# Cross-attention K and V as split float32r products, a ctx tile read twice through one buffer, and a new order of work on all five queues

## The reference, cut to what matters

```
# layer 0: attention of x over ctx (16 heads of 16), relu projections, row mask, layernorm
q, k, v = relu(x@Wq+bq), relu(ctx@Wk+bk), relu(ctx@Wv+bv)
x  = layernorm(softmax(mask(q k^T / 4)) v + x) * gamma + beta
# layer 1: a Mamba2 block, then cross-attention over the same ctx (8 heads of 32)
zxbcdt = rms(x) @ in_proj                  # 256 -> 1288
xBC = silu(conv4(xBC));  y = scan over t of h = h*decay + u*B, y = h.C
h  = x + rms(y * silu(z)) @ out_proj
q1 = layernorm(h) @ Wq1;  k1 = ctx @ Wk1;  v1 = ctx @ Wv1
out = h + (softmax(q1 k1^T / sqrt(32)) v1) @ Wo
```

## Time and profile before

| | us |
|---|---|
| median of three runs | 1428.14 |
| profiled execution, time | 1427.8 |
| profiled execution, span | 1426.0 |
| TensorE busy | 1329.9 (93%) |
| VectorE busy | 1267.2 (89%) |
| ScalarE busy | 1089.3 (76%) |
| GpSimd busy | 891.7 (63%) |

### The profile page before, as it was taken

One profiled execution on the slowest core, in us unless ns is written; L12 is line 12 of the kernel. 1 busy time (PEld: TensorE's weight loads), 2 busy tenths in 40 slices (PEclk: granted clock), 3 DMA queues, 4 the chain that ended last, 5 costly groups with the idle time before them and its releaser, 6 DMA issues.

```text
span 1426.0 us, 42008 instructions
## 1 busy us (share of the span) xinstructions
PE 1329.9 (93%) x15112; PEld 1160.4 (81%) x15112; DVE 1267.2 (89%) x3050; ACT 1089.3 (76%) x3300; POOL 891.7 (63%) x1125
## 2 busy tenths in 40 slices
PE   4799999999999999999999999999999999999875
PEld 3688888888888888888888888888888888888764
DVE  5799999999999999998899999998989999999872
ACT  3667787887778788778778778877877878877653
POOL 6366666567666666665656766666666665676642
PEclk9999999999999999999999999999999999999997
DMA  5021121211222111122221122211122211201110
GB/s 190 25 66 63 64 72 58 72 51 39 72 72 72 58 50 54 57 72 72 57 71 52 39 72 72 72 57 50 47 63 72 72 58 60 60 26 54 46 46 15
DMA packets 41132, 86.91 MB, mean 61 GB/s; under 512 B 5728, under 2 KB 10976, under 8 KB 40928
## 3 DMA queue, kind: packets, MB, share of 16 engines
q1 hardware_dynamic: 39632, 81.96, 17.9%
q10 hardware_dynamic: 1296, 2.27, 0.5%
HBM read 75.53 MB, written 8.68 MB: 59 GB/s over the span
## 4 chain that ended last, share of the span: by engine, by line
PE 72%; DVE 11%; POOL 8%; issue 4%; DMA 3%; ACT 1%; SPq 1%; POOLq 0%; DVEq 0%; ACTq 0%
PE bank L294 19%; PE bank L397 9%; PE bank L522 8%; POOL PC L1548 6%; PE bank L535 5%; PE bank L354 5%; PE bank L508 4%; PE bank L387 4%; PE bank L573 4%; PE bank L411 4%; DVE stc L957 3%; DMA cU<-in_cT 3%; PE bank L593 2%; PE bank L622 2%; PE bank L445 2%
## 5 line engine op out<-in xcount | busy, mean ns | idle before, releaser
L848 DVE SCALAR_TENSOR_TENSOR ACC<-bank,cw,ACC 128x250 f32<-128x250 f32 (+2 forms) x576 | 270.3, 473 | 10.4
L1548 POOL TENSOR_TENSOR PC<-PC,stc 128x512 f32<-128x512 f32 x128 | 191.1, 1494 | 78.0 <-DVE stc L964 78.0
L1351 ACT ACTIVATE PC<-bank,stc 128x128 f32<-128x128 f32 x512 | 180.9, 380 | 66.8 <-DVE stc L957 66.8
L1188 ACT ACTIVATE PTA<-bank 128x512 f32<-128x512 f32 x256 | 142.2, 599 | 82.3 <-PE bank L391 80.1
L294 PE MATMUL bank<-xnT,wnl 128*128 128x256 f32 x640 | 199.2, 311 | 0.3 <-DVE xnL L783 0.3
L294 PE MATMUL bank<-xnL,wnh 128*128 128x256 f32 x640 | 179.4, 280 | 0.0
L294 PE MATMUL bank<-xnT,wnh 128*128 128x256 f32 x640 | 179.1, 280 | 0.0
L707 DVE TENSOR_REDUCE sta<-bank 128x4 f32<-128x512 f32 x256 | 160.8, 681 | 8.1 <-PE bank L354 5.6
L872 DVE TENSOR_TENSOR_SCAN L<-DB,id 128x1024 f32<-128x1024 f32 x64 | 146.1, 2282 | 0.0
L522 PE MATMUL bank<-wout,Y 128*128 128x256 f32 x512 | 123.9, 386 | 6.4 <-POOL SQ L1526 6.4
L1489 POOL TENSOR_SCALAR stn<-stn 128x1 f32<-128x1 f32 x64 | 15.2, 238 | 173.2 <-ACT junk L1207 173.2
(11 more groups left out here) (182 smaller groups left out, 4247.7 us busy)
## 6 DMA issues: line engine op xcount, KB each, us to landing
DB<-dec_scratch SPq DMA_DIRECT2D x64, 512.0 KB, 4.5
xT<-in_xT SPq DMA_DIRECT2D x32, 256.0 KB, 2.7
cT<-in_cT SPq DMA_DIRECT2D x32, 256.0 KB, 2.9
xt<-in_xt SPq DMA_DIRECT2D x32, 256.0 KB, 2.7
cU<-in_cT SPq DMA_DIRECT2D x32, 256.0 KB, 4.3
...
```

The lines of the kernel that those rows point to most:

```text
L848: e.scalar_tensor_tensor(out=w, in0=t[:, 0:T].rearrange("p (b t) -> p b t", b=NB)[:, :, 0:125 + k], scalar=cw[:, c, k:k + 1], in1=w, op0=A ...
L1188: e.activation(PTA[n % 4][:, :, :], t[:, :].rearrange("p (i k) -> p i k", i=4), ACT.Exp).then_inc(s_eA, 1)
L1351: op = e.activation(PC[n % 5][:, p, :], t[:, p * 128:(p + 1) * 128], ACT.Exp, bias=stc[g % 4][:, 4 * i + p:4 * i + p + 1], accum_out=stc[g ...
L1548: e.tensor_tensor(PC[n % 5][:, :, :], PC[n % 5][:, :, :], stc[g % 4][:, 16 + 4 * i:20 + 4 * i].unsqueeze(2).to_broadcast([128, 4, 128]), A ...
```

## The change

1. `k1` and `v1` become split products of three: weights `wk1h`/`wk1l`, `wv1h`/`wv1l`, data `cUh`/`cUl`. `k1` calls `proj3`; `v1` issues twelve float32r matmuls instead of four float32 ones.
2. `cU` is gone. ctx is still loaded twice per group, both times into the one buffer `cT`: `load_c(g)` for layer 0, and `load_u(g)` three groups behind it (`AHEAD`). ScalarE gets `split_u`, GpSimd `lo_u`.
3. The two weights are split once: ScalarE at its step 2, GpSimd at its step 17. They are staged in `HT`, and `wq1u` in `OT`; three buffers go, and the ring `PC` has four instead of five.
4. `nm` keeps its first instruction; the second is `nw`, which can stand later in the list.
5. `USES` and all five lists are replaced. In the lists of ScalarE, GpSimd and SyncE some offsets are larger by a constant; only the order within a queue counts. `later` on GpSimd now stands before the first `qm`, where it stood one step behind it.

```diff
+AHEAD = 3
@@ load_c, load_u
             def load_c(g):
                 if ok(g) and g > 0:
                     e.wait_ge(s_cl, g)
+                    if g > AHEAD:
+                        e.wait_ge(s_ul, g - AHEAD)
                     e.dma_start(cT[:, :, :], a["cT"][g]).then_inc(d_cT, 16)
...
             def load_u(g):
                 if ok(g):
+                    e.wait_ge(s_cl, min(g + AHEAD + 1, NG))
                     if g > 0:
-                        e.wait_ge(s_v1p, g)
-                        e.wait_ge(s_k1p, 2 * g)
-                    e.dma_start(cU[:, :, :], a["cT"][g]).then_inc(d_cU, 16)
+                        e.wait_ge(s_ul, g)
+                    e.dma_start(cT[:, :, :], a["cT"][g]).then_inc(d_cU, 16)
@@ the queue of SyncE, one step
-                load_t(s - 7)
-                dec_in(s - 9, 1)
-                load_x(s - 5)
-                load_c(s - 5)
-                dec_out(s - 8)
-                store(s - 11)
-                load_m(s - 5)
-                load_u(s - 7)
-                dec_in(s - 8, 0)
+                load_m(s - 13)
+                load_c(s - 13)
+                store(s - 20)
+                load_u(s - 16)
+                load_x(s - 12)
+                dec_in(s - 16, 1)
+                load_t(s - 14)
+                dec_out(s - 15)
+                dec_in(s - 15, 0)
@@ k1, v1
-                        e.wait_ge(d_cU, 16 * (g + 1))
-                    full(t, 0, wk1, m, cU).then_inc(s_k1p, 1)
+                        e.wait_ge(s_ul, g + 1)
+                    proj3(t, 0, wk1h, m * 128, cUh, cUl, wk1l).then_inc(s_k1p, 1)
...
                     for b in range(NB):
+                        n = 0
                         for kk in range(2):
-                            mm = e.matmul(t[:, b * 256:(b + 1) * 256], cU[:, kk, b * 128:(b + 1) * 128], wv1[:, kk, :],
-                                          start=(kk == 0), stop=(kk == 1))
+                            for w, c in ((wv1l, cUh), (wv1h, cUl), (wv1h, cUh)):
+                                mm = e.matmul(t[:, b * 256:(b + 1) * 256], c[:, kk, b * 128:(b + 1) * 128], w[:, kk, :],
+                                              start=(n == 0), stop=(n == 5))
+                                n += 1
@@ VectorE: the second piece of the maxima
-                    e.wait_ge(s_nm, 2 * ns + 1)
-                    e.tensor_tensor(NM[ns % 2][:, :, 4:8], w, NM[ns % 2][:, :, 0:4].bitcast(F32), ALU.subtract).then_inc(s_nm, 1)
+
+            def nw(g, b):
+                if ok(g):
+                    ns = 2 * g + b
+                    w = sta[ns % 4][:, 0:16].rearrange("p (j i) -> p j i", j=4)
+                    e.wait_ge(s_nm, ns + 1)
+                    e.tensor_tensor(NM[ns % 2][:, :, 4:8], w, NM[ns % 2][:, :, 0:4].bitcast(F32), ALU.subtract).then_inc(s_nw, 1)
@@ the new ctx split
+            def split_u(g):
+                if ok(g):
+                    e.wait_ge(d_cU, 16 * (g + 1))
+                    if g > 0:
+                        e.wait_ge(s_v1p, g)
+                        e.wait_ge(s_k1p, 2 * g)
+                    e.activation(cUh[:, :, :], cT[:, :, :], ACT.Copy).then_inc(s_uh, 1)
+            def lo_u(g):
+                if ok(g):
+                    e.wait_ge(s_uh, g + 1)
+                    e.tensor_tensor(cUl[:, :, :], cT[:, :, :], cUh[:, :, :].bitcast(F32), ALU.subtract).then_inc(s_ul, 1)
@@ GpSimd, before its first step with work
-                if s == 1:
+                if s == 16:
                     late()
-                if s == 2:
+                if s == 16:
                     later()
+                if s == 17:
+                    for i, (hi, lo) in enumerate(((wk1h, wk1l), (wv1h, wv1l))):
+                        e.wait_ge(z_1h, i + 1)
+                        e.tensor_tensor(lo[:, :, :], w1[i], hi[:, :, :].bitcast(F32), ALU.subtract).then_inc(z_1l, 1)
```

More of the change, by code:

```diff
@@ L100, in program @@
         NT = ring("NT", 2, [128, 4, 128], F32R)
-        PC = ring("PC", 5, [128, 4, 128])
+        PC = ring("PC", 4, [128, 4, 128])
         PTC = ring("PTC", 4, [128, 4, 128])
@@ L201, in program @@
         stage = [XC[k][:, :, :].rearrange("p c t -> p (c t)")[:, 0:NPROJ] for k in range(2)]
+        wq1u = OT[:, :, :].rearrange("p (a b) c -> p a (b c)", a=2)
+        w1 = [HT[i][:, :, :] for i in range(2)]
         bvr, negm = xh[0], xh[1][:, 0:128]
@@ new lines, in tensor @@
+                av(s - 3, 1)
+                av(s - 3, 2)
+                av(s - 3, 3)
+                sT(s - 3, 1)
+                ot(s - 3, 0)
+                k(s - 2, 1)
+                bx(s - 4, 0)
+                av(s - 3, 4)
+                av(s - 3, 5)
+                av(s - 3, 6)
+                av(s - 3, 7)
+                tC(s - 6, 0)
+                gm(s - 4, 0)
+                ht(s - 5, 0)
+                q(s - 1, 0)
+                sA(s - 2, 0)
+                ot(s - 3, 1)
@@ new lines, in tensor @@
+                q(s - 1, 1)
+                k1(s - 5, 1)
+                tC(s - 6, 1)
+                k(s - 1, 0)
+                v(s - 1, 0)
+                ht(s - 5, 1)
+                sA(s - 2, 1)
+                y(s - 4, 0)
+                tC(s - 6, 2)
+                bx(s - 4, 1)
+                q1(s - 5, 0)
+                q1(s - 5, 1)
+                tC(s - 6, 3)
+                nt(s - 3, 0)
+                gm(s - 4, 1)
+                sC(s - 5, 0)
+                y(s - 4, 1)
@@ new lines, in vector @@
+                xc(s - 4, 3)
+                tap(s - 4, 14)
+                tap(s - 4, 15)
+                rC(s - 6, 2)
+                tap(s - 4, 16)
+                tap(s - 4, 17)
+                xc(s - 4, 4)
+                hm(s - 5, 1)
+                rC(s - 6, 3)
+                xc(s - 4, 5)
+                rc(s - 3, 0)
+                xo(s - 3, 0)
+                scan(s - 4, 0)
+                bs(s - 3, 0)
+                lg(s - 4, 0)
+                mA(s - 2, 0)
+                rc(s - 3, 1)
@@ new lines, in vector @@
+                mA(s - 2, 6)
+                scan(s - 4, 1)
+                lg(s - 4, 1)
+                mC(s - 5, 0)
+                nl(s - 3, 0)
+                nl(s - 3, 1)
+                yd(s - 4, 1)
+                mC(s - 5, 1)
+                mC(s - 5, 2)
+                mA(s - 2, 7)
+                d0(s - 3, 0)
+                nm(s - 2, 1)
+                d0(s - 3, 1)
+                tap(s - 3, 0)
+                tap(s - 3, 1)
+                dc(s - 3, 0)
+                tap(s - 3, 2)
@@ new lines, in vector @@
+                dc(s - 3, 1)
+                dc(s - 3, 2)
+                r1(s - 4, 0)
+                dc(s - 3, 3)
+                xc(s - 3, 0)
+                hh(s - 4, 0)
+                dc(s - 3, 4)
+                dc(s - 3, 5)
+                hs(s - 4, 0)
+                dc(s - 3, 6)
+                dc(s - 3, 7)
+                dc(s - 3, 8)
+                nw(s - 2, 1)
+                rC(s - 5, 0)
+                hg(s - 4, 0)
+                dc(s - 3, 9)
+                dc(s - 3, 10)
@@ new lines, in vector @@
+                mC(s - 5, 3)
+                tap(s - 3, 3)
+                dc(s - 3, 11)
+                rC(s - 5, 1)
+                sz(s - 3, 0)
+                fin(s - 6, 0)
+                sz(s - 3, 1)
+                tap(s - 3, 4)
+                r1(s - 4, 1)
+                dk(s - 3, 0)
+                hm(s - 4, 0)
+                tap(s - 3, 5)
+                hh(s - 4, 1)
+                tap(s - 3, 6)
+                xc(s - 3, 1)
+                tap(s - 3, 7)
+                tap(s - 3, 8)
@@ L1121, in scalar @@
+                hs(s - 4, 1)
+                tap(s - 3, 9)
+                hg(s - 4, 1)
         def scalar(e):
@@ new lines, in scalar @@
+                zt(s - 4, 1)
+                da(s - 4, 0)
+                eC(s - 6, 3)
+                ac(s - 4, 2)
+                th(s - 4, 1)
+                hx(s - 5, 0)
+                eA(s - 3, 0)
+                eA(s - 3, 1)
+                ac(s - 4, 3)
+                eA(s - 3, 2)
+                th(s - 4, 2)
+                ac(s - 4, 4)
+                eA(s - 3, 3)
+                ac(s - 4, 5)
+                th(s - 4, 3)
+                nt_(s - 3, 1)
+                th(s - 4, 4)
```

409 lines of the change are left out of this document (151 added, 258 removed), and 22 rows, old and new, of the table USES.

## The result

Six runs of the changed kernel have a median of 1434.35 us (1433.47 to 1439.59), six of the kernel before beside them 1428.51. The ratio is 1.0044, 95% interval 1.0027 to 1.0061: slower by 0.4%, where 1410 was forecast. The profiled execution took 1433.96 us, and its span is 1432.2, 6.2 more than before.

The account below looks back on a forecast made before the run. TensorE was taken as the bound, VectorE close behind. Per step 42.12 - 0.34 - 1.23 + 0.76 = 41.31 us; 26 us less over 32 steps, 6 more at the start and small allowances gave 1410 us, range 1396 to 1422.

Parts of the forecast that it names:

- K and V in split form: TensorE's k1 and v1 as float32r products: net 0.34 us saved per step, ends 0.68 and 0.
- The lock goes: TensorE's tC no longer waits for GpSimd's nC, held by VectorE's scan: 1.23 us of idle time per step go.
- One buffer for both ctx tiles: SyncE's load_u waits for lo_c with dec_in(.,1) queued behind; it fits by 1.8 us, so nothing counted.
- fourth rival: Shared cT makes dec_in late by 1 us beyond its margin: step 42.31, 1440 us; chance 0.06.
- What is late next: Second scan on VectorE waits for GpSimd's ga, so the second y starts 0.76 us late every step; ends 0 and 1.80.
- VectorE's dependent steps: Fewer dependent neighbours in VectorE's list: 1.4 us less load per step, counted as no time because TensorE is busy longer.
- third rival: VectorE's distances are fixed whether neighbours depend or not: step stays 42.12, 1434 us with the start; chance 0.06.
- Start: later before the first qm on GpSimd delays group 0's first layer-0 scores by 7.9 us: +6, between 0 and 8.
- Sum: Adding the terms: step 41.31 us, 26 us less over 32 steps, 6 more at the start; forecast 1410 us.

Follow-up runs that it names:

- g_pe: On a3_lx, v1 keeps only one of its three products, so TensorE does 0.94 us less per step; 1426.47 us, ratio 0.9973.
- d_tapin: On a3_lx, VectorE's convolution taps 10, 13 and 16 work on 4 columns a sequence instead of 126; 1421.18 us, ratio 0.9953.
- a3_lx: The changed kernel with load_x in front of load_u on SyncE's queue; 1419.95 us, ratio 0.9938 to the kernel before.
- b_cutin: The changed kernel with z(.,0) and cp(.,1) keeping one of three products, 1.4 us less on TensorE per step; 1427.77 us, ratio 0.9983.
- g_both: On a3_lx, the cuts of g_pe and d_tapin together; 1416.57 us, ratio 0.9917.

## Why the prediction was wrong, step by step

The forecast step was 41.31 us and the measured one 42.11, some 25 us over 32 steps. Two of its steps failed: that the 1.23 us of idle time would go with the lock, and that the shared buffer would cost nothing.

**K and V in split form** held. -0.34 per step was forecast; undoing the split costs 0.42 and 0.44, inside the ends of 0 and 0.68. In the step shown, `k1` takes 718.06 - 717.35 = 0.71.

**The lock goes** failed in what it did to the sum. `tC` no longer waits and `nC` is 1.04, but the 1.23 of idle time did not go: 0.69 of it came back as the wait for `cL`, and some 0.2 as transposes that wait for ScalarE (2.4 + 2.0 us, six times), at least in part where `xT` is late. The prediction looked for the lock at the second scan only. In the new list `xo` stands right in front of the first, so GpSimd's `xr` meets it in every step.

**One buffer for both ctx tiles** is the step whose failure cost most. It named `load_x` as queued behind `load_u` and then worked out the margin of `dec_in` alone. That one did not run out, though both its sums were short: in the step shown `dec_in` goes out at 720.19, 5.9 us behind the end of the first scan, since the two `nC` and the rest of `xr` stand in between, and with 4.7 for the landing that makes 10.6 instead of 6.8; the second scan comes after 11.5 instead of 8.6. `load_x` had no margin: ScalarE waited for it 29 times, 39.5 us in all. Moving it one place gave 14.4 us, more than the whole loss of 6. The fourth rival had the place, but named the wrong transfer and gave it 0.06.

**What is late next**, +0.76, had the right size: 0.80. The mechanism was half right. The forecast had `ga` first and the scan waiting. In most steps of the changed kernel the scan is first, and the second `y` waits for the `xd` behind `ga`; with `load_x` moved it is as forecast, 3.04 for the scan. The Trainium skill, page "SBUF — State Buffer", section "SBUF: two separate sides", says that whichever instruction starts first keeps the other out for its whole length. The runs agree in both directions: `ga` 3.01 behind a scan, the scan 3.04 behind `ga`.

**VectorE's dependent steps** were mis-sized. 1.4 us less were forecast, and busy time did fall by 1.15, from 38.85 to 37.70, but most of that is something else. Taken one by one, VectorE's instructions are 21.1 us shorter in 27 steps, which is 0.78 a step: `x2` and the first piece of the maxima were held before and are held less now (total us, then mean ns; before, then after).

```profile
L769 DVE SCALAR_TENSOR_TENSOR X<-xa,sta,bet 128x256 f32<-128x256 f32 x54 | 37.7, 698 | 0.0
L719 DVE CAST NM<-sta 128x16 fp32r<-128x16 f32 x54 | 28.5, 529 | 0.0
```

```profile
L785 DVE SCALAR_TENSOR_TENSOR X<-xa,sta,bet 128x256 f32<-128x256 f32 x54 | 25.7, 480 | 0.0
L730 DVE CAST NM<-sta 128x16 fp32r<-128x16 f32 x54 | 17.6, 326 | 0.6 <-issue 0.6
```

Only 0.37 is left for neighbours that overlap more. The same list of VectorE is busy for 38.74 in g_pe, where L775 is held, so busy time is no measure of the distances. That the term brings no time by itself was right (d_tapin).

The third rival's 1434 is the measured time, but its mechanism is not what kept the step at 42.1: the waits for `cL`, for the second `y` and for `xT` did, and a3_lx, with the same list of VectorE, is 14.4 us shorter. The size of the term itself was measured by no run.

**Start**: +6 was forecast, the first scan is 7.9 late and the span 6.2 longer. The delay that it was worked out from is real in part: `later` holds the first scores back by 5.0 us. But moving `later` back gains 1.5 at the first `xr` and nothing in the time, and 4.4 come from TensorE's order, which the forecast left out. The number was right by luck.

**Sum.** By what was measured: 42.12 - 0.50 (TensorE's busy time) - 1.22 (waits for `nC` and `cU`) + 0.69 + 0.80 + 0.2 = 42.1. The forecast of 41.31 lacked the last 0.2 and the 0.69 (and had 0.34 in place of the 0.50). Its method was at fault as well: it took each term as time. In b_cutin 1.4 us less on TensorE is worth 0.24 on the most frequent step, and in g_both 0.9 less on each of two queues 0.19. Which path sets the remaining 41.4 us was not settled.
